# Softmax sums of an attention kernel: GpSimd powers of minus one in place of VectorE reciprocals

## The reference

```python
xn = group_norm(x, gn_gamma, gn_beta)
qkv = jnp.einsum('bchw,oc->bohw', xn, w_qkv).reshape(B, 3, nh, d, H * W)
q, k, v = (qkv[:, 0], qkv[:, 1], qkv[:, 2])
scores = jnp.einsum('bhci,bhcj->bhij', q, k) * d ** (-0.5)
attn = jax.nn.softmax(scores, axis=-1)
out = jnp.einsum('bhij,bhcj->bhci', attn, v).reshape(B, C, H, W)
proj = jnp.einsum('bchw,oc->bohw', out, w_proj) + b_proj[None, :, None, None]
return xn + proj
```

## Time and profile before

| | us |
|---|---|
| median of 3 runs | 5567.9 |
| lowest and highest of them | 5565.55, 5569.24 |
| span of the profiled execution | 5568.2 |
| steps of the first image's attention (141 to 1363) | 1222 |
| steps of the second image's attention (1541 to 2761) | 1220 |
| everything after the attention (2806 to 5568) | 2762 |

### The profile page before, as it was taken

The page is one execution under the profiler, slowest core; times in us unless marked ns, Lnnn a source line. Parts: engine busy times, 40 slices in busy tenths (PEclk is TensorE's granted clock), DMA queues, the critical chain, the costliest instruction groups (busy, mean ns, idle before and its releaser), DMA issues. The chain is left out here.

```text
span 5568.2 us, 75691 instructions
## 1 busy us (share of the span) xinstructions
PE 5050.2 (91%) x23148; PEld 2344.5 (42%) x23148; DVE 4172.1 (75%) x6834; ACT 2291.1 (41%) x4176; POOL 3191.6 (57%) x2819
## 2 busy tenths in 40 slices
PE   7999999999799999999978869969997996999688
PEld 3333333333333333333336657645543553555344
DVE  4888888885488888888633334448986896888898
ACT  2444444443244444444401112125544554555455
POOL 0666666656056666666617757746555663665675
PEclk9999999999899999999978879979998998999899
DMA  2000000000100000000034435559987998999999
GB/s 72 1 1 1 1 1 1 1 1 2 61 1 1 1 1 1 1 1 1 1 92 124 127 103 159 162 205 374 370 332 296 383 377 309 375 388 359 381 410 359
DMA packets 320281, 812.36 MB, mean 146 GB/s; under 512 B 70094, under 2 KB 137556, under 8 KB 319758
## 3 DMA queue, kind: packets, MB, share of 16 engines
q0 software_dynamic: 193536, 679.59, 32.4%
q1 hardware_dynamic: 126478, 129.39, 6.8%
HBM read 708.40 MB, written 100.43 MB: 145 GB/s over the span
## 5 line engine op out<-in xcount | busy, mean ns | idle before, releaser
L638 POOL TENSOR_TENSOR arena<-arena 128x512 f32<-128x512 f32 x960 | 1406.1, 1465 | 828.9 <-ACT arena L1265 764.4
L1265 ACT ACTIVATE arena<-ps 128x1024 f32<-128x1024 f32 x1024 | 1049.6, 1025 | 1239.4 <-PE ps L816 1209.9
L1788 DVE TENSOR_REDUCE arena<-ps 128x2 f32<-128x1024 f32 x1024 | 1243.1, 1214 | 347.3 <-PE ps L790 347.2
L690 POOL DMA_INDIRECT arena<-corners,arena x1152 | 1092.4, 948 | 694.5 <-issue 303.1
L2018 DVE SCALAR_TENSOR_TENSOR ps<-arena,ps 128x256 f32<-128x256 f32 x2304 | 955.8, 483 | 235.6 <-DVEq L2012 226.4
L1139 PE MATMUL ps<-arena 128*128 128x512 f32 x2304 | 1050.4, 599 | 0.2
L816 PE MATMUL ps<-arena 64*128 64x512 f32 x4096 | 1046.0, 589 | 0.0
L829 PE MATMUL ps<-arena 128*64 128x512 f32 x4096 | 991.3, 605 | 0.0
L1810 DVE TENSOR_TENSOR arena<-arena 128x512 f32<-128x512 f32 x960 | 888.6, 926 | 62.5 <-ACT arena L1265 62.1
L674 POOL DMA_INDIRECT arena<-corners,arena x576 | 545.0, 946 | 275.1 <-issue 243.9
L1450 ACT ACTIVATE ps<-arena 128x256 f32<-128x256 f32 x1152 | 499.2, 469 | 453.3 <-DMA arena<-corners,arena 198.7
(11 more groups left out here) (161 smaller groups left out, 3777.0 us busy)
## 6 DMA issues: line engine op xcount, KB each, us to landing
corners<-arena SPq DMA_DIRECT2D x256, 256.0 KB
arena<-corners,arena POOLq DMA_INDIRECT x1728, 9.0
img<-in_x SPq DMA_DIRECT2D x8, 1024.0 KB, 9.3
corners<-arena SPq DMA_DIRECT2D x128, 64.0 KB, 2.2
arena<-in_wd SPq DMA_DIRECT2D x2, 2304.0 KB, 8.9
between<-img SPq DMA_DIRECT2D x4, 1024.0 KB, 6.3
arena<-between SPq DMA_DIRECT2D x4, 1024.0 KB, 10.0
resid<-img SPq DMA_DIRECT2D x8, 512.0 KB
```

The lines of the kernel that those rows point to most:

```text
L638: pool.tensor_tensor(SUMS[u % 2][:, 0, :], SUMS[u % 2][:, 0, :], P[n % 4][:, 0, :], ALU.add).then_inc(sum_a, 1)
L690: pool.indirect_dma_start(G3[4 * k + t].rearrange("p a c -> p (a c)"), None, table256[b], bass.IndirectOffsetOnAxis(ap=IS3[:, k, t:t + 1], ...
L1265: af(P[n % 4].rearrange("p h q -> p (h q)"), ps[:, 2 * (n % 2):2 * (n % 2) + 2, :].rearrange("p h q -> p (h q)"), ACT.Exp, scale=float(D) ...
L1788: v.tensor_reduce(mxp[i % 2][:, :, j], ps[:, 4:6, :], AX.X, ALU.max).then_inc(mx_done, 1)
```

## The change

The inversion of `RC` moves from DVE to POOL. DVE loses its eight reciprocals of 128x64 for a block. POOL gets four `tensor_tensor` instructions of 128x128 for a block, which raise `RC` to the power of a new tile `MINUS` that holds -1. They stand after the adds of steps 10, 11, 12 and 13 of the next block; those of the last block stand after its last add, in a row, ahead of the last `normalized`. A memset of `MINUS` is added for each image.

```diff
+        MINUS = att.f32(128)
...
-                for what, value in ((COEF, 0.0), (MSTAT, 0.0), (ONES, 1.0)):
+                for what, value in ((COEF, 0.0), (MSTAT, 0.0), (ONES, 1.0), (MINUS, -1.0)):
...
+                def inverse_sums(u, i):
+
+                    pool.wait_ge(aux_done, aux_at[("sums", u)] + 1)
+                    pool.tensor_tensor(RC[:, i * 128:(i + 1) * 128], RC[:, i * 128:(i + 1) * 128], MINUS,
+                                       ALU.pow).then_inc(rc_done, 1)
+
                 def normalized(u):
 
-                    pool.wait_ge(rc_done, 8 * (u + 1))
+                    pool.wait_ge(rc_done, 4 * (u + 1))
                     pool.wait_ge(o_done, u + 1)
...
+                    if 10 <= kc < 14 and u >= 1:
+                        inverse_sums(u - 1, kc - 10)
                     if kc == 16 and u >= 1:
                         normalized(u - 1)
+                for i in range(4):
+                    inverse_sums(BLOCKS - 1, i)
                 normalized(BLOCKS - 1)
...
-                def inverse_sums(u, i):
-
-                    dve.wait_ge(aux_done, aux_at[("sums", u)] + 1)
-                    v.reciprocal(RC[:, i * 64:(i + 1) * 64], RC[:, i * 64:(i + 1) * 64]).then_inc(rc_done, 1)
-
...
-                    if g >= NT // 2 and 3 <= g % (NT // 2) <= 6:
-                        inverse_sums(g // (NT // 2) - 1, 2 * (g % (NT // 2) - 3))
                     add_b(2 * g)
-                    if g >= NT // 2 and 3 <= g % (NT // 2) <= 6:
-                        inverse_sums(g // (NT // 2) - 1, 2 * (g % (NT // 2) - 3) + 1)
                 add_b(STEPS - 1)
-                for i in range(8):
-                    inverse_sums(BLOCKS - 1, i)
```

More of the change, by code:

```diff
@@ L436, in _ @@
                 sp.sem_inc(at_done, -BLOCKS)
-                sp.sem_inc(rc_done, -8 * BLOCKS)
+                sp.sem_inc(rc_done, -4 * BLOCKS)
                 go()
@@ L594, in _ @@
                 inverse_root(grs[:, :])
-                for what, value in ((COEF, 0.0), (MSTAT, 0.0), (ONES, 1.0)):
+                for what, value in ((COEF, 0.0), (MSTAT, 0.0), (ONES, 1.0), (MINUS, -1.0)):
                     pool.memset(what, value).then_inc(pool_step, 1)
-                pool.wait_ge(pool_step, 3)
-                pool.sem_inc(pool_step, -3)
+                pool.wait_ge(pool_step, 4)
+                pool.sem_inc(pool_step, -4)
                 for h in range(2):
```

## The result

| | before | after |
|---|---|---|
| median, us | 5566.73 (4 runs) | 7773.18 (4 runs) |
| lowest to highest, us | 5564.73 to 5569.24 | 7769.47 to 7776.99 |
| span of the profiled execution, us | 5568.2 | 7775.2 |

The changed kernel takes 1.3965 times as long (95% interval 1.3946 to 1.3983): 2206 us more. The forecast was 7898 us.

What follows compares the result with a forecast made beforehand. PE was taken to bound the steps, with DVE close to the bound. 5568 us plus 2231 for thirty blocks plus 99 for two image ends gave 7898 us; the 8-in-10 range was 5750 to 8050.

Steps and rivals of the forecast that it cites:

- The price of a power: On POOL, 0.562 us plus 150 ns for each further column, so 19.6 us for each 128x128 power; chance 0.50.
- The rival of a better rate on long rows: POOL's columns overlap on long rows: at a quarter rate 5.3 us a power, 6027 us in all; chance 0.33.
- the cheap power: Rival: a power costs about an add, 0.88 us, and fits POOL's free time; 5501 us in all; chance 0.15.
- What the removal gains: Eight reciprocals fewer on DVE gain 2.24 us a block, 67 us over thirty blocks; nothing at the images' ends.
- what stands on DVE is paid in full: In the steps, DVE is so close to the bound that anything put between its maxima and adds costs its full time.
- Whom a power holds up: POOL's and DVE's adds wait for a power, then maxima and PE's leading scores; the kernel stands within about one step.
- the sum without the rule: If powers do not block DVE's adds, buffers `P` stall ACT some three steps later; about 7 us a block less lost.
- The sum for a block: Powers and adds 83.9 us, less 9.1 for steps, plus 1.8 for clock: 76.6 lost, 74.4 after the 2.24 gain.
- the four steps that were to be made beside four powers: From the first power's start to the fourth's end, four steps of 2.28 us proceed, offsetting 9.1 us a block.
- what stands between them: Between a block's four powers, three POOL adds of 1.26 us and three DVE waits of 0.55 us: 5.4 us.
- the 1.8 us for the clock: PE restarts at 1.2 GHz behind the fourth power: 3.6 us do 1.8 us of work, losing 1.8 us.
- The ends: At each image's end the projection's eighth chunk waits 47.6 us for `normalized`, plus 1.8 for clock: 49.4, 99 for two.

Runs made afterwards that it cites:

- the sizes measured one by one: Changed kernel with fourteen more POOL instructions, powers of 64x1 to 128x128 and products of 128x1 to 128x512, behind the first image's last block: 7802.0 us.
- the product: Changed kernel with a product in place of each power, same operands, pieces and places, leaving the inversion out: 5510.69 us, 0.9896 times the time before.
- the thin reciprocals: Kernel before with DVE's reciprocals in sixteen pieces of 32 columns over pairs 3 to 13, `normalized` after step 30: 5523.18 us, 0.9917.
- the ends alone: Kernel before with the four powers on POOL for each image's last block only, other blocks keeping DVE's reciprocals: 5682.15 us.
- the powers further apart: Changed kernel with a block's four powers after steps 8, 14, 20 and 26, and `normalized` after step 28: 7531.82 us.

## Why the prediction was right, point by point

*The price of a power* was the choice that carried the forecast, and it was right: 19.6 us forecast, 20.8 measured. It was a choice, with a chance of one half, and no row of the trace before could have settled it. The one column between the two sizes of the earlier trace rows gave the rate for 128 columns within 6%. The rival of a better rate on long rows falls by the sizes measured one by one, and the cheap power with it. That partitions do not count was shown as well.

*What the removal gains:* 67 us forecast, 62 in the steps with the product. The sum took fifteen blocks of each image; the last of them has no maxima any more, and lost nothing before: from its first exponential to its last it takes 63.8 us before and with the product alike, while a block in the middle takes 77.5 and 75.2. That what stands on DVE is paid in full, as the prediction says, does not hold for small pieces: the thin reciprocals are 5.3 us of DVE a block and cost the steps 5 us of a whole image.

*Whom a power holds up:* here the prediction's mechanism was wrong. DVE's adds do not wait for a power as they do for POOL's adds. The rule of the Trainium skill ("SBUF — State Buffer", "Who interferes with whom"), by which the second instruction fully blocks, agrees with the adds and not with the powers: adds begun at 392.06 and 413.26, within a power, take 0.68 and 0.69 us. The measurement decides, and the sum without the rule, which the prediction set about 7 us a block lower, was the better one.

*The sum for a block:* 76.6 us lost before the gain, measured 69.9 + 2.1 = 72.0 (the 2.1 are the 62 us shared among thirty blocks). The mis-sized term is the four steps that were to be made beside four powers. It was six, in every one of the thirty blocks: from the start of the first power to the end of the fourth (389.99 to 476.72) ACT begins three steps ahead of its first wait and one behind each of the first three powers. Six steps of 2.28 us are 13.7 us in place of 9.1. Three more terms were off. The powers take 4.8 us more; what stands between them takes 3.5 us in place of 5.4, since DVE's adds are not in that path; and the 1.8 us for the clock do not show (below). 76.6 + 4.8 - 1.9 - 4.6 - 1.8 = 73.1; the last 1.1 us stay open. The errors partly cancel, so it is in part luck that the forecast came within 125 us. Of these, the blocks are 30 x 4.5 = 135 less, the ends 11 more.

*The ends:* 49.4 us forecast, 54.8 in the profile, 56.5 with the ends alone. Four powers take 83.0 us in place of 78.4, which is most of it.

*The clock:* stretches from within the first power to behind the fourth, in the view of the earlier trace rows:

```profile
404.50:418.00 13.50, 4.72 (x14) 1.58 (x16) 1.92 (x2) 1.02 (x1) 13.50 (x3) 0.50 0.00 0
418.10:421.40 3.30, 1.13 (x6) 0.10 (x2) 0.00 (x0) 0.00 (x0) 3.30 (x1) 1.00 0.00 0
421.50:462.40 40.90, 7.49 (x20) 2.24 (x22) 3.92 (x5) 2.05 (x2) 40.90 (x5) 0.50 0.00 0
...
466.00:482.80 16.80, 3.60 (x12) 1.60 (x14) 2.46 (x3) 3.07 (x3) 16.51 (x6) 0.50 0.00 0
483.00:500.00 17.00, 17.00 (x91) 5.78 (x89) 15.46 (x15) 7.34 (x8) 15.28 (x11) 1.00 0.00 0
```

The granted clock is at the lower level, 1.2 GHz, for most of the powers and up to 482.8, behind the last, and full speed is there from 483 on, as forecast. Within the second power it is at full speed for 3.3 us, after PE has worked from 413.28 on; the same comes back from 462.5 to 465.8, within the fourth, and not within the third. The cost was not the one forecast. From 391.65 to the first exponential behind the fourth power, at 478.12, six steps take 86.5 us where 13.7 is usual: 72.8 lost. From there to 487.13 four steps take 9.0 us, where 9.1 is usual. So nothing is seen to be lost behind the fourth power, where the prediction puts 1.8 us; whether full speed would have won something back there is not shown. At the ends it is 6.09 - 3.70 = 2.4 us, against 1.8.

## What to carry to other kernels

An operation that looks like its neighbours can be 47 times as dear. Two small rows of it gave the rate to within 6% here, and the rate decided; that the rate holds on long rows was known only once several sizes had been measured. Ask then who waits for the engine that gets the work: here each engine had free time as an average, but four buffers were worth three steps, and a piece nine steps long stood in the way of an add that all others needed. The same work fitted on ACT, which sits idle 2.46 us in most pairs, in pieces of 1.28 us and less.

## What was not expected of the hardware

A power keeps DVE's adds from SBUF only in its first part. An add begun 0.17 us into a power of 128x128 (389.99) ends at 390.99, 1.00 us after the power's start; one begun 0.18 us into a power of 128x512 (394.24) ends at 396.07, 1.83 after it. Less the 0.55 us that an add takes once it gets through the earlier trace rows, it was let in some 0.45 and 1.28 us behind the power's start. With the powers further apart, adds begin at other moments:

```profile
518.97 0.93 DVE L1821 TENSOR_TENSOR arena<-arena 128x512 f32<-128x512 f32 x1
```

This one begins 0.08 us into the power at 518.89 and ends 1.01 us after its start. Fifty adds of that run begin 0.02 to 0.32 us into a power, and all end 1.00 us after its start, within 0.01; those begun later take their usual 0.68 to 0.71. A product of these sizes takes 0.44 and 1.25 us in all. So it looks as if the power reads its operands at a product's pace and computes the rest of its 20.8 or 82.2 us without SBUF's reads. That is inferred from these times, for two sizes; no run here shows the reads themselves.
